# State-space layer and expert layer in one kernel: a new slot table for the work around the scan

## What is computed

```python
xn = x * rsqrt(mean(x * x) + EPS) * norm_w            # x: layer-normed input
x_inner, gate = split(xn @ in_proj_w)
xc = causal_conv4(x_inner * silu(gate))
dt = softplus(xc @ dt_w + dt_b)
Bm, Cm = xc @ B_w, xc @ C_w
h[t] = exp(dt * A) * h[t-1] + dt * Bm * xc            # per channel and state
y = sum_s h * Cm + D_skip * xc
out = y @ out_proj_w

top_v, top_i = top_k(x @ gate_w, 2); top_p = softmax(top_v)
expert = sum_k top_p[k] * (silu(x @ Wg[e]) * (x @ Wu[e])) @ Wd[e]
shared = silu(x @ Sg) * (x @ Su) @ Sd                  # 352 columns
```

## Time and profile before

| | us |
|---|---|
| median of 3 runs (1847.18 to 1849.93) | 1848.69 |
| the profiled execution | 1850.68 |
| its span | 1849.1 |
| TensorE matmul busy | 1594.4 (86%) |
| VectorE busy | 1172.0 (63%) |
| GpSimd busy | 1039.0 (56%) |
| ScalarE busy | 859.0 (46%) |

### The profile page before, as it was taken

The page is one execution under the profiler, slowest core; times in us unless marked ns, Lnnn a source line. Parts: engine busy times, 40 slices in busy tenths (PEclk is TensorE's granted clock), DMA queues, the critical chain, the costliest instruction groups (busy, mean ns, idle before and its releaser), DMA issues. The chain is left out here.

```text
span 1849.1 us, 23292 instructions
## 1 busy us (share of the span) xinstructions
PE 1594.4 (86%) x6828; PEld 1030.2 (56%) x6828; DVE 1172.0 (63%) x1953; ACT 859.0 (46%) x1498; POOL 1039.0 (56%) x1192
## 2 busy tenths in 40 slices
PE   5788798898998998998997685478999999999990
PEld 2344555554644645645555454356777777777770
DVE  1298999898999898998989993122222222222225
ACT  3566658567667567576575562111212212122124
POOL 0568778778778788788788872312222222222224
PEclk9899999999999999999999887689999999999996
DMA  3111112111211121111112111178212222122116
GB/s 94 47 35 47 47 45 84 64 55 43 70 52 47 64 59 46 64 58 53 52 47 69 41 46 47 58 257 260 35 32 33 33 35 33 33 35 33 33 30 187
DMA packets 82983, 115.65 MB, mean 63 GB/s; under 512 B 10992, under 2 KB 56912, under 8 KB 82864
## 3 DMA queue, kind: packets, MB, share of 16 engines
...
## 5 line engine op out<-in xcount | busy, mean ns | idle before, releaser
L894 POOL TENSOR_TENSOR bb<-u,br 128x512 f32<-128x512 f32 x512 | 646.4, 1274 | 183.0 <-DVE hh L749 180.7
L615 ACT ACTIVATE bA<-dt,a_neg 128x512 f32<-128x512 f32 x512 | 353.5, 692 | 294.7 <-DVE hh L749 289.2
L480 PEld LDWEIGHTS bH<-ident,hh 128*128 128x128 f32 x2048 | 254.4, 146 | 304.0 <-issue 154.8
L480 PE MATMUL bH<-ident,hh 128*128 128x128 f32 x2048 | 324.6, 284 | 74.7 <-DVE hh L749 60.4
L749 DVE TENSOR_TENSOR_SCAN hh<-bA,bb 128x512 f32<-128x512 f32 x256 | 306.5, 1210 | 46.4 <-ACT bA L615 36.0
L749 DVE TENSOR_TENSOR_SCAN hh<-bA,hl,bb 128x512 f32<-128x512 f32 x256 | 322.5, 1271 | 17.7 <-ACT bA L615 17.7
L766 DVE SCALAR_TENSOR_TENSOR yT<-bH,bc,yT 128x512 f32<-128x512 f32 x360 | 262.8, 730 | 35.0 <-PE bH L480 34.4
L1260 POOL DMA_INDIRECT sum_scratch<-yt,xt x71 | 113.3, 1595 | 189.2 <-issue 151.5
L1295 ACT ACTIVATE sgm<-bG 128x352 f32<-128x352 f32 x142 | 58.1, 461 | 326.6 <-PE bG L1120 326.6
L1163 PE MATMUL bD<-w_d,hT 128*128 x852 | 198.4, 383 | 0.8 <-ACT hT L1301 0.8
...
L1120 PE MATMUL bG<-w_g,xtT 128*128 x568 | 181.6, 463 | 2.7 <-DMA w_d<-in_L_ffn_Wd_dram 2.2
...
## 6 DMA issues: line engine op xcount, KB each, us to landing
br<-b_scratch SPq DMA_DIRECT2D x128, 256.0 KB, 3.2
...
```

The costliest lines, as they stand in the source:

```text
L480: i = e.transpose(bH[g % NH][:, q * P:(q + 1) * P], hh[:, (n - 1) % 2, q, d * P:(d + 1) * P], ident[:])
L615: e.activation(bA[g % NA][:], dt[c % 2][:, d, :], ACT.Exp, scale=a_neg[:, d, n:n + 1]).then_inc(s_a, 1)
L894: e.tensor_tensor(bb[:, k % NB, :], u[c % 2][:, d, :], br[:, n % NR, :], ALU.mult).then_inc(s_bb, 1)
```

## The change

Four things, in words, and the core of the diff behind them.

- **The shared expert's silu** becomes one instruction over sgs (1536 columns, the unused partitions zeroed once) at SLOTS + 13, ahead of the gates' silu of another chunk in the same slot, and loads no table of its own behind it where that one follows. For chunk 5, which has no gates beside it, and chunks 6 and 7 (`LATE`) it stands alone; chunk 7's is not followed by a load.
- **Its up and down products** go from slots 57 to SLOTS + 6 to SLOTS + 34 to SLOTS + 45, the copies and the store with them; sg2 shares slots 54 and 55 with sg1. Chunk 6 keeps up products at 59 to 63 and has its down products at SLOTS + 24 in the drain, into hs. For chunk 7 rank comes ahead of sg and the multiplications by su behind the position.
- **One-hot rows** are made on GpSimd, in a subtraction and a comparison with zero over 64 elements, in place of two VectorE comparisons; the two reductions to posf become one.
- **Norms** are done by row tile, one in each of four slots (58 to 61, 30 to 33, 43 to 46), and so is the add to x (31 to 34).

Besides, gates, y2, inner3, dt1 and dt2 move by some slots, all slot numbers stand in tables, and waits that named the last of several banks now name them all (`all_emptied`, `all_filled`).

```diff
-PROJ = {"gate0": 0, "gate1": 2, "gate2": 9, "gate3": 11, "inner0": 13, "inner1": 15, "inner2": 17, "inner3": 19,
-        "cv0": 21, "cv1": 24, "cv2": 27, "cv3": 30, "bT": 33, "dt0": 36, "bc": 38, "dt1": 40, "dt2": 44, "dt3": 49}
-POST = {"y0": 4, "y1": 6, "y2": 7, "y3": 8, "out0": 10, "out1": 16, "xfT0": 47, "xfT1": 48, "logit": 51, "sg0": 52, "sg1": 54, "sg2": 56,
-        "su0": 57, "rank": 58, "su1": 59, "su2": 63, "sd0": SLOTS + 3, "sd1": SLOTS + 5}
-POST_END = SLOTS + 12
+PROJ = {"gate0": 0, "gate1": 5, "gate2": 7, "gate3": 11, "inner0": 13, "inner1": 15, "inner2": 17, "inner3": 20, "cv0": 21, "cv1": 24, "cv2": 27,
+        "cv3": 30, "bT": 33, "dt0": 36, "bc": 38, "dt1": 41, "dt2": 46, "dt3": 49}
+POST = {"y0": 4, "y1": 6, "y2": 3, "y3": 8, "out0": 10, "out1": 16, "xfT0": 47, "xfT1": 48, "logit": 51, "rank": 58, "sg0": 52, "sg1": 54, "sg2": 54,
+        "su0": SLOTS + 36, "su1": SLOTS + 34, "su2": SLOTS + 40, "sd0": SLOTS + 42, "sd1": SLOTS + 44}
+
+ACT_AT = {"gate": (2, 7, 9, 13), "silu": 13, "conv": (24, 27, 30, 32), "bT": 36, "bc": 39, "dt": (40, 44, 48, 53), "root_x": 52,
+          "norm_x": (58, 59, 60, 61), "xnT": (62, 63), "out": (14, 20), "root_out": 25, "norm_out": (30, 31, 32, 33), "root_xf": 39,
+          "xf": (43, 44, 45, 46), "xfT": (48, 49), "e2": 58, "sg": (54, 56, 56), "sg_silu": SLOTS + 13, "sd": (SLOTS + 44, SLOTS + 46), "sum": 3}
+DVE_AT = {"stats_x": 48, "inner": (16, 18, 20, 21), "y": (5, 7, 4, 9), "stats_out": (16, 22), "stats_xf": 36, "logit": 52, "max": 53, "index": 54,
+          "place": 59, "base": 60, "position": 62, "sgs": (SLOTS + 37, SLOTS + 35, SLOTS + 41)}
+POOL_AT = {"var_x": 50, "norm_x": 53, "halo": 5, "dt": (43, 47, 51, 55), "var_out": 24, "norm_out": 28, "add": (31, 32, 33, 34), "var_xf": 38,
+           "norm_xf": 41, "diff": 55, "token": 50, "chosen": 57, "picked": 61, "gates": SLOTS, "scatter": SLOTS + 2}
+
+LATE = {("sg_silu", NCH - 2): 58, ("su0", NCH - 2): 59, ("su1", NCH - 2): 60, ("su2", NCH - 2): 62, ("sgs", NCH - 2): (60, 61, 63),
+        ("sd0", NCH - 2): SLOTS + 24, ("sd1", NCH - 2): SLOTS + 26, ("sd", NCH - 2): (SLOTS + 26, SLOTS + 28),
+        ("rank", NCH - 1): 52, ("sg0", NCH - 1): 53, ("sg1", NCH - 1): 55, ("sg2", NCH - 1): 57, ("e2", NCH - 1): 53, ("sg", NCH - 1): (55, 57, 59), ("sg_silu", NCH - 1): 60,
+        ("su0", NCH - 1): 60, ("su1", NCH - 1): 61, ("su2", NCH - 1): 63, ("sgs", NCH - 1): (SLOTS + 1, SLOTS + 1, SLOTS + 1),
+        ("sd0", NCH - 1): SLOTS + 3, ("sd1", NCH - 1): SLOTS + 5, ("sd", NCH - 1): (SLOTS + 5, SLOTS + 7)}
...
+def slot(table, name, c):
+    return LATE.get((name, c), table[name])
...
+        def sh(c):
+            return hs[:].rearrange("p i (j d) -> p (i j) d", d=DM) if c == NCH - 2 else on[:]
...
-            if k == 32:
-                e.wait_ge(s_o3, c + 1)
-                for j in range(J):
-                    i = e.activation(on[:, j, :], on[:, j, :], ACT.Identity, scale=r2[:, j:j + 1], bias=nmr2[:, j:j + 1])
-                i.then_inc(s_on, 1)
-            if k == 39:
+            for j in range(J):
+                if k == ACT_AT["norm_out"][j]:
+                    e.wait_ge(s_o3, c + 1)
+                    e.activation(on[:, j, :], on[:, j, :], ACT.Identity, scale=r2[:, j:j + 1], bias=nmr2[:, j:j + 1]).then_inc(s_on, 1)
...
-            if k == 58:
-                emptied(e, "sg2", c)
-                for t, (i0, n) in enumerate(SIT):
-                    e.activation(sgs[0:n, t, :], sgs[0:n, t, :], ACT.Silu).then_inc(s_ssil, 1)
-                e.preload_act_table_set(LOGEXP)
+            if k == slot(ACT_AT, "sg_silu", c):
+                all_emptied(e, ["sg0", "sg1", "sg2"], c)
+                e.activation(sgs[:].rearrange("p s t -> p (s t)"), sgs[:].rearrange("p s t -> p (s t)"), ACT.Silu).then_inc(s_ssil, 1)
+                if NCH - 4 < c < NCH - 1:
+                    e.preload_act_table_set(LOGEXP)
             for h in range(2):
-                if k == SLOTS + (5, 7)[h]:
+                if k == slot(ACT_AT, "sd", c)[h]:
                     filled(e, f"sd{h}", c)
-                    e.wait_ge(s_x1, c + 1)
-                    e.copy(sh[:, 2 * h:2 * h + 2, :].rearrange("p j d -> p (j d)"), at(f"sd{h}", c)[:]).then_inc(freesem(f"sd{h}", c), 1)
-            if k == SLOTS + 7:
+                    if c == NCH - 2:
+                        e.wait_ge(s_ya, NS * NCH)
+                    else:
+                        e.wait_ge(s_x1, J * min(c + 2, NCH))
+                    e.copy(sh(c)[:, 2 * h:2 * h + 2, :].rearrange("p j d -> p (j d)"), at(f"sd{h}", c)[:]).then_inc(freesem(f"sd{h}", c), 1)
+            if k == slot(ACT_AT, "sd", c)[1]:
                 emptied(e, "sd0", c)
                 emptied(e, "sd1", c)
-                e.dma_start(rows_of(sh_d, c), sh[:]).then_inc(s_shs, 16)
+                e.dma_start(rows_of(sh_d, c), sh(c)).then_inc(s_shs, 16)
...
-            if k == 56:
-                e.wait_ge(s_cr, 4 * c + 3)
-                for kk in range(TOPK):
-                    i = e.tensor_tensor(oh[:, kk, :, :], iota_e[:].unsqueeze(1).broadcast_to([P, J, E]),
-                                        ixf[:, :, kk:kk + 1].broadcast_to([P, J, E]), ALU.is_equal)
-                i.then_inc(s_cr, 1)
...
-            if k == 55:
-                e.wait_ge(s_cr, 4 * c + 2)
+            if k == slot(POOL_AT, "diff", c):
+                e.wait_ge(s_cr, 2 * c + 2)
                 e.tensor_tensor(dif[:], mx[:, :, 1], mx[:, :, 0], ALU.subtract)
-                e.tensor_copy(ixf[:], ix[:, :, 0:TOPK]).then_inc(s_cr, 1)
-            if k == 50:
+                e.tensor_copy(ixf[:], ix[:, :, 0:TOPK].rearrange("p j k -> p k j")).then_inc(s_ch, 1)
+                e.wait_ge(s_ch, 3 * c + 1)
+                each = [P, TOPK * J, E]
+                oh8 = oh[:].rearrange("p k j e -> p (k j) e")
+                e.tensor_tensor(oh8, iota_e[:].unsqueeze(1).broadcast_to(each), ixf[:].rearrange("p k j -> p (k j)").unsqueeze(2).broadcast_to(each),
+                                ALU.subtract).then_inc(s_ch, 1)
+                e.wait_ge(s_ch, 3 * c + 2)
+                e.tensor_scalar(oh8, oh8, 0.0, None, ALU.is_equal).then_inc(s_ch, 1)
...
-            if k == 33:
-                e.wait_ge(s_on, c + 1)
-                e.wait_ge(s_xr, 16 * (c + 1))
-                e.tensor_tensor(xr[:].rearrange("p j d -> p (j d)"), xr[:].rearrange("p j d -> p (j d)"),
-                                on[:].rearrange("p j d -> p (j d)"), ALU.add).then_inc(s_x1, 1)
...
+                if k == POOL_AT["add"][j]:
+                    e.wait_ge(s_on, J * c + j + 1)
+                    e.wait_ge(s_xr, 16 * (c + 1))
+                    e.tensor_tensor(xr[:, j, :], xr[:, j, :], on[:, j, :], ALU.add).then_inc(s_x1, 1)
...
```

More of the change, by code:

```diff
@@ L61, in bank_table @@
         for k in range(SLOTS):
-            for names, c, slot in ((POST, loop - 2, SLOTS + k), (PROJ, loop + 1, k), (POST, loop - 1, k), (LEAD, loop + 2, k)):
-                turn += [(name, c) for name, at in names.items() if at == slot and 0 <= c < NCH]
+            for names, c, now in ((POST, loop - 2, SLOTS + k), (PROJ, loop + 1, k), (POST, loop - 1, k), (LEAD, loop + 2, k)):
+                turn += [(name, c) for name in names if 0 <= c < NCH and slot(names, name, c) == now]
     return {use: (i % NQ, i // NQ + 1) for i, use in enumerate(turn)}
@@ L262, in summed, with all_emptied, all_filled @@
                 e.wait_ge(s_hs, m // J + 1)
+        def all_emptied(e, names, c):
+            for b in range(NQ):
+                n = max([PLACE[name, c][1] for name in names if PLACE[name, c][0] == b], default=0)
+                if n:
+                    e.wait_ge(free[b], n)
+        def all_filled(e, names, c):
+            for b in range(NQ):
+                n = max([PLACE[name, c][1] for name in names if PLACE[name, c][0] == b], default=0)
+                if n:
+                    e.wait_ge(full[b], n)
+        GATES, INNERS, CONVS = ([f"{name}{d}" for d in range(ND)] for name in ("gate", "inner", "cv"))
+        def sh(c):
+            return hs[:].rearrange("p i (j d) -> p (i j) d", d=DM) if c == NCH - 2 else on[:]
         def rows_of(d, c):
@@ L415, in pe_post @@
                 b = f"xfT{h}"
-                if k == POST[b]:
+                if k == slot(POST, b, c):
                     e.wait_ge(s_xf, J * (c + 1))
@@ L446, in pe_post @@
             for t, (i0, n) in enumerate(SIT):
+                b = f"sg{t}"
+                q = k - slot(POST, b, c)
+                if 0 <= q < KD:
+                    if q == 0:
+                        room(e, b, c)
+                    i = e.matmul(at(b, c)[0:n, :], w_sg[:, q, i0:i0 + n], xfT[:, q, :], start=(q == 0), stop=(q == KD - 1))
+                    if q == KD - 1:
+                        i.then_inc(fullsem(b, c), 1)
+            for t, (i0, n) in enumerate(SIT):
                 b = f"su{t}"
-                q = k - POST[b]
+                q = k - slot(POST, b, c)
                 if 0 <= q < KD:
```

(12 more changed lines are left out.)

187 lines of the change are left out of this document (92 added, 95 removed).

## The result

The changed kernel takes 1880.7 us (median of 4 runs, 1877.2 to 1884.1) where the kernel before took 1848.2 beside it: a ratio of 1.018, 95% interval 1.0158 to 1.0202. It is 32 us slower. The prediction, 1836 in a range of 1817 to 1858, was wrong. The profiled execution took 1884.1, its span is 1882.1 (before 1849.1).

A forecast was written before the change was run, and what follows sets the result against it. VectorE was taken to pace the loop, with TensorE close behind. The terms summed to -12.9 us, from the profiled 1850.7 to 1837.8, less 2.0 to the median: 1836 us, range 1817 to 1858.

The forecast's parts named there:

- Slots 32 to 55: the price: Up and down products moved here make TensorE the bound: 53.3 us a loop, +28 us over loops 2 to 6.
- lead of 1.0: Slots 32 to 55: 1.0 us of TensorE's lead carries over, taken off each loop's time.
- Silu: Slot 13: the added silu lengthens VectorE's wait by 1.5 us in loops 2 to 6, +7.5; loop 7 +2.0.
- forecast case: Whole kernel: the summed terms hold, 1836 us, from 1827 to 1847 by their bounds; chance 0.38.
- rival (a): Slots 14 and 49: TensorE waits, then its clock drops to 1.2 GHz; +30 us, 1866; chance 0.24.
- One-hot rows and end of loop: One-hot rows off VectorE: -12.4 us; slots 56 to 63, loops 1 to 6, fewer waits and multiplications: -24.0.
- Cost 0: GpSimd's two one-hot operations, 0.3 us each, cost nothing, or 0.6 per loop where GpSimd is late.
- Slots 0 to 11: Down products and one multiplication leave, VectorE's waits mostly for bH shrink: -10.1 us.
- Drain: After the last scan: posl about 8 us earlier, padi deciding and 3.8 later; -7.7 us, bounds -3 and -11.
- Norms by row tile: Slots 32 and 45: about 0.3 us spared in a loop, GpSimd's four adds cost as much; 0.
- Other loops: Loop 7: silu wait +2.0 us, sgs multiplications 1.8; loops 0 and 1: dt2's bank, 1.0 each.

The follow-up runs named there:

- e7_down_third: Changed kernel, two of three contraction pieces of the shared expert's down products left out for chunks 0 to 5: 1863.2 us, ratio 1.0086.
- e12: Changed kernel with the one-hot rows back on VectorE at slot 56: 1887.2 us, ratio 1.0198.
- e6: Kernel before the change with only the one-hot rows moved to GpSimd: 1855.3 us, ratio 1.005.
- e11: Changed kernel with shared expert, gates, inner3, y2 and dt in their old slots and one-hot rows on VectorE: 1832.6 us, ratio 0.99.
- e2_split_silu: Changed kernel with the shared silu alone at slot 58 with its own table loads, products staying late: 1883.2 us, ratio 1.0184.

## Why the prediction was wrong, point by point

Profiled span against profiled span the change cost 33.0 us where the steps gave -12.9. Phase 2, unchanged, has 3.2 of the 33.0. In loops 2 to 6 the steps gave -5.6 (with each loop's waits as they were read) and 37.5 came: the misses are 17.5 in slots 32 to 55, 14.6 in slots 12 to 31, 6.1 in slots 0 to 11 and 4.9 at the end of the loop.

- **Slots 32 to 55: the price** failed, and weighs most: +28 predicted, +45.5 measured (53.3 us per loop against 57.0). That TensorE becomes the bound was right, and e7_down_third shows it. The count of its work was nearly right too (53.2, and 53.95 busy), though the same count for the kernel before, 41.1, is 2.2 under its 43.33. Wrong were its own waits, 1.1 predicted and 3.05 measured: beside dt2's bank (1.36) there are the transposes of xf behind the norms by tile (0.99), conv's copy (0.33) and B's (0.37). And there was no lead of 1.0 to carry over.
- **Silu** failed: +7.5 predicted, +22.1 in slots 12 to 31. The size of the added instruction, 1.49, and VectorE's wait behind it, 3.99, were right to 0.1. The step that failed is that this wait was taken for all that the block costs. What was left out of the forecast case is rival (a): TensorE, blocked by the same block, comes back at 1.2 GHz. I had put a drop at about 2 us of TensorE work; in four of five loops slots 16 to 19 lose 1.6 to 2.7. Slots 12 to 15, at 0.88 to 0.90 in the same four loops, lose 11.7 in the five, 4 more than the block's length. The other place of rival (a), slot 49, did not show: the clock is 1.00 in all of slots 32 to 55.
- **One-hot rows and end of loop**: -30.6 for loops 2 to 6, -25.7 measured. In the changed kernel the move itself is worth 7.5 of its 10.3 (e12). On the kernel before it was worth nothing (e6). "Cost 0" for GpSimd was right for the two operations (0.29 and 0.38) and wrong for what stands behind them.
- **Slots 0 to 11**: -10.5 for the five loops, -4.4 measured. The waits for bH mostly went, as said. Three waits for hl at slot 8 of the even loops, 2.0 us together before, grew to 9.5 (the longest 4.1): GpSimd's copy stands behind the scatters there, and VectorE now comes sooner.
- **Drain**: -7.7 predicted, -10.2 measured, inside its bounds. posl came earlier by 12 instead of 8, and padi, said to be what decides, did decide: the pads wait 2.22 for it. It came 1.0 earlier, where the steps had it 1.9 later.
- **Norms by row tile**, put at 0 (0.3 us a loop, and as much lost by GpSimd's adds): 9.2 us in the five loops in slots 32 to 55 where the slots of before are kept (e11 against before). In the changed kernel TensorE binds there and the gain does not show.
- **Other loops**: loop 0 +2.5, loop 1 -4.7 (predicted +1.0 and -3.8), loop 7 +5.0 (predicted +3.2).

Rival (a) named the right side and, for slot 14, the right mechanism; its 1866 fell short by 15. The point from which it decides, 55.9 us per loop in slots 32 to 55, was passed (57.0), though by TensorE's work and waits and not by its clock.

The Trainium skill (ScalarE: Activation LUTs, What ACT_TABLE_LOAD costs) gives 2.66 us for a switch to another table. Here the measurement differs and decides: the loads took 1.28, and the next instruction began 1.3 behind their start. e2_split_silu has ten more loads than the kernel after, 12.8 us of ScalarE by the rows, and took 2.5 us more in all; that does not price them, as its silu moved with them and two stretches changed by 19 us each. The Trainium skill (TensorE: Matmul & The Clock Gate, HAM oscillation) describes turns of waiting and slow running, and the rows of slots 13 to 19 agree: a wait of 3.15 us, then a granted clock of 0.51.

Still open: how the 22 us at slots 12 to 31 divide exactly between the clock and the block's own waits (8.6 are in slots 16 to 19, where TensorE is busy throughout); whether other work for TensorE under ScalarE's block would keep the clock up (not tried); why phase 2 varies by 9 us; and the two groups of e6_onehot_only.
